# Maxima and exponentials of opposite row halves in turn, and three and two PSUM banks for them

## What is computed

```
xn = layernorm(x)
x + attn(xn) + ffn(xn)

attn: 16 heads of 8; softmax attention in chunks of 16 tokens, once on neighbours,
      once on every third token; the sum of both through Wo
ffn:  y  = xn + mla(rmsnorm(xn, w_ln1))          16 heads, causal, 512 x 512 scores
      y + moe(rmsnorm(y, w_ln2))                 1 shared and 7 routed experts, top 2

mla:  scores = einsum('bqhd,bkhd->bhqk', qq, kk) * scale, masked where k > q
      probs  = softmax(scores);  y = einsum('bhqk,bkhd->bqhd', probs, v) @ W_o
```

## Time and profile before

| | us |
|---|---|
| median of 3 runs | 514.09 |
| lowest, highest | 512.26, 516.3 |
| the profiled execution | 514.96 |
| its span on the chip | 513.0 |

### The profile page before, as it was taken

The page is one execution under the profiler, slowest core; times in us unless marked ns, Lnnn a source line. Parts: engine busy times, 40 slices in busy tenths (PEclk is TensorE's granted clock), DMA queues, the critical chain, the costliest instruction groups (busy, mean ns, idle before and its releaser), DMA issues.

```text
span 513.0 us, 11641 instructions
## 1 busy us (share of the span) xinstructions
PE 464.1 (90%) x4428; PEld 244.8 (48%) x4428; DVE 361.0 (70%) x1049; ACT 265.1 (52%) x486; POOL 53.2 (10%) x52
## 2 busy tenths in 40 slices
PE   3774988999999999999999997999999999987995
PEld 2322343445453555545455554454545545654652
DVE  6463586687767877776577784666677775688886
ACT  6252447457766554877754385776543444212110
POOL 4231001141001121010002120000010000010000
PEclk9868699999999999999999997999999999999899
DMA  6156000156000227100001264000400000000000
GB/s 206 24 137 116 0 3 2 21 127 134 3 2 3 65 56 134 27 3 2 2 3 34 54 125 68 1 3 2 125 1 4 2 1 22 0 22 1 1 20 21
DMA packets 18198, 20.22 MB, mean 39 GB/s; under 512 B 2824, under 2 KB 16392, under 8 KB 17352
## 3 DMA queue, kind: packets, MB, share of 16 engines
q1 hardware_dynamic: 18144, 19.49, 17.4%
HBM read 10.84 MB, written 7.47 MB: 36 GB/s over the span
## 4 chain that ended last, share of the span: by engine, by line
PE 60%; DVE 20%; DMA 6%; issue 5%; ACT 5%; SPq 3%; POOL 1%; DVEq 0%; ACTq 0%; POOLq 0%
PE bank_A L1080 7%; PE bank_c L1043 6%; PE bank_A L1001 6%; PE bank_B L1026 6%; PE bank_M L1091 6%; DVE x L942 4%; PE bank_B L1124 4%; DMA q_stack<-in_c_rows 4%; PE bank_M L1098 4%; DVE k_diag L922 3%; PE bank_B L1031 3%; PE bank_M L985 3%; DVE k_diag L927 3%; PE bank_A L1130 2%; SPq L478 2%
## 5 line engine op out<-in xcount | busy, mean ns | idle before, releaser
L672 ACT ACTIVATE p_mla<-bank_B 128x512 f32<-128x512 f32 (+1 forms) x176 | 97.5, 561 | 92.9 <-PE bank_B L1031 91.4
L819 DVE CUSTOM_DVE_ANT_0 differences<-masks,bank_A 128x384 bf16<-128x384 bf16 (+1 forms) x128 | 78.4, 613 | 25.2 <-PE bank_A L1001 20.2
L651 ACT ACTIVATE pT_loc<-sT_loc 32x512 f32<-32x512 f32 x136 | 85.1, 625 | 4.8 <-DVE sT_loc L845 3.4
L1001 PE MATMUL bank_A<-k_stack,q_stack 50*128 50x128 bf16 (+3 forms) x256 | 65.2, 307 | 11.0 <-DMA q_stack<-in_c_rows 7.4
L1124 PE MATMUL bank_B<-xrT,k_diag 128*128 128x512 f32 x128 | 64.4, 617 | 3.9 <-DVE k_diag L922 3.2
L1026 PE MATMUL bank_B<-q_stack,k_stack 50*128 50x512 bf16 (+3 forms) x256 | 63.9, 302 | 0.6 <-DVE k_diag L922 0.2
L838 DVE TENSOR_REDUCE row_max<-bank_A 128x16 f32<-128x512 f32 (+1 forms) x36 | 24.8, 690 | 40.7 <-PE bank_A L1080 40.6
L1080 PE MATMUL bank_A<-k_diag,qT 128*32 128x512 f32 x272 | 50.5, 772 | 0.0
L1031 PE MATMUL bank_B<-masks 64*128 64x64 bf16 (+1 forms) x512 | 50.3, 202 | 0.0
L1043 PE MATMUL bank_c<-p_mla,v_mla 128*9 128x128 f32 (+3 forms) x512 | 47.5, 442 | 0.4 <-ACT p_mla L672 0.3
L1031 PEld LDWEIGHTS bank_B<-masks 64*128 64x128 bf16 x512 | 39.8, 95 | 14.3 <-issue 0.2
(11 more groups left out here) (135 smaller groups left out, 593.3 us busy)
## 6 DMA issues: line engine op xcount, KB each, us to landing
parts_dram<-parts SPq DMA_DIRECT2D x16, 192.0 KB, 2.7
k_stack<-parts_dram SPq DMA_DIRECT2D x8, 384.0 KB
q_stack<-parts_dram SPq DMA_DIRECT2D x8, 384.0 KB
parts_dram<-parts SPq DMA_DIRECT2D x16, 128.0 KB, 2.7
k_diag<-kT SPq DMA_DIRECT2D x64, 18.0 KB
x<-in_x SPq DMA_DIRECT2D x4, 256.0 KB, 6.6
parts_dram<-parts SPq DMA_DIRECT2D x16, 64.0 KB, 2.3
out<-x SPq DMA_DIRECT2D x4, 256.0 KB, 2.2
```

The lines of the kernel that those rows point to most:

```text
L651: last = nc.scalar.activation(pT_loc[rows, :, rows], sT_loc[rows, t % 2, :].rearrange("p (h k) -> p h k", h=H), ACT.Exp, scale=SCALE)
L672: drained_by(nc.scalar.activation(p_mla[:, n % P_RING, m:m + len(heads), j * P:], src, ACT.Exp, scale=SCALE), step)
L819: drained_by(nc.vector.tensor_tensor_reduce(differences[:, 0:w], masked16[:, S - w:], bank[:, 0:w], -1.0, -NEG, ALU.add, ALU.min, dst), step)
L1001: last = nc.tensor.matmul(bank[:, n * w:(n + 1) * w], q_stack[b % 2][rows, h % 8, i * P:(i + 1) * P], k_stack[b % 2][rows, h % 8, 0:w], st ...
```

## The change

Ring A gets three banks and ring B two. The groups go in the order 0, 1, 2, 3 and a group's maxima units start with the widest tile, so that its 11 units have the same widths and head counts, one by one, as its 11 exponential units. The lists of maxima and exponentials become one, `scores`, over all 16 groups, spread evenly from -0.29 to 4.0: unit k of group n's maxima stands directly before unit k of the exponentials of group n - 2, followed by a PV where one is due. SHIFT of a group comes after the second unit of the next. `merged` takes such a bundle as one entry, so no other step comes between its parts.

On TensorE, where an exponential unit directly follows a maxima unit (`beside`), the maxima step only waits for its bank. The exponential step waits for its own and then issues both: exponential matmul of a head, maxima matmul of a head, in turn, and after them the masks in turn. The outputs and the norm of the third batch are placed somewhat later. No matmul, drain or DMA is added or taken away. The helpers `exp_matmul`, `exp_mask` and `half_of` (not shown) issue the matmuls of L1026 and L1031 with their operands as before.

```diff
--- before
+++ after
-BANKS = {"A": 2, "B": 3, "M": 2}
+BANKS = {"A": 3, "B": 2, "M": 2}
...
-GROUP_ORDER = [0, 2, 1, 3]
+GROUP_ORDER = [0, 1, 2, 3]
+LEAD = 2
...
 def score_units():
     units = []
     for g in GROUP_ORDER:
-        for i in range(NT):
+        for i in reversed(range(NT)):
...
-    "latent": [(0, 1.12), (1.12, 2.02), (2.02, 2.86), (2.86, 4)],
-    "maxima": [(-0.29, 0.63), (0.61, 1.44), (1.56, 2.46), (2.49, 3.54)],
+    "scores": [(-0.29, 4.0)],
...
-    "outputs": [(1.18, 1.34), (2.12, 2.26), (2.86, 2.97), (4.02, 4.27)],
-    "norm": [(1.31, 1.53), (2.33, 2.54), (3.17, 3.65), (4.28, 4.57)],
+    "outputs": [(1.18, 1.34), (2.13, 2.26), (3.08, 3.19), (4.02, 4.27)],
+    "norm": [(1.31, 1.53), (2.33, 2.54), (3.26, 3.65), (4.28, 4.57)],
...
-    def maxima(b):
-        steps = []
-        for n, g in enumerate(GROUP_ORDER):
-            steps += [("S", b, u) for u in range(PER_GROUP * n, PER_GROUP * n + PER_GROUP)] + [("SHIFT", b, g)]
-        return steps
-
-    def latent(b):
-        steps, late = [], []
-        for g in GROUP_ORDER:
-            for j in range(NT):
-                units = [("E", b, g, j, u) for u in range(len(exp_units(g, j)))]
-                steps += units[:1] + late + units[1:]
-                late = [("PV", b, g, j)]
-        return steps + late
+    def scores():
+
+
+        groups = [(b, g) for b in range(B) for g in GROUP_ORDER]
+        found, shift, late = [], [], []
+        for n in range(len(groups) + LEAD):
+            here = groups[n] if n < len(groups) else None
+            back = groups[n - LEAD] if n >= LEAD else None
+            exps = [("E",) + back + (j, u) for j in range(NT) for u in range(len(exp_units(back[1], j)))] if back else []
+            for k in range(PER_GROUP):
+                unit = []
+                if here:
+                    unit.append(("S", here[0], PER_GROUP * GROUP_ORDER.index(here[1]) + k))
+                if back:
+                    unit.append(exps[k])
+                found.append(unit + late + (shift if k == 1 else []))
+                late = []
+                if back and (k + 1 == PER_GROUP or exps[k + 1][3] != exps[k][3]):
+                    late = [("PV",) + exps[k][1:4]]
+            shift = [("SHIFT",) + here] if here else []
+        return found + [late]
...
-    lists = [(experts(range(B)), *at["experts"][0])]
+    lists = [(experts(range(B)), *at["experts"][0]), (scores(), *at["scores"][0])]
     for b in range(B):
-        lists += [(latent(b), *at["latent"][b]), (maxima(b), *at["maxima"][b]), (local(b), *at["local"][b]),
+        lists += [(local(b), *at["local"][b]),
                   (outputs(b), *at["outputs"][b]), (norm(b), *at["norm"][b]), ([("ST", b)], *at["stacks"][b]),
...
+    beside = {e: s for s, e in zip(steps, steps[1:]) if (s[0], e[0]) == ("S", "E")}
+    waits_for_e = set(beside.values())
...
+            def maxima_matmul(step, n):
+                b, (i, heads) = step[1], UNITS[step[2]]
+                h, w = heads[n], (i + 1) * P
+                rows = slice(half_of(h).start, half_of(h).start + STACK_ROWS)
+                return nc.tensor.matmul(bank_of(step)[:, n * w:(n + 1) * w],
+                                        q_stack[b % 2][rows, h % 8, i * P:(i + 1) * P],
+                                        k_stack[b % 2][rows, h % 8, 0:w], start=n == 0, stop=i >= 2,
+                                        skip_group_check=True)
+
+            def maxima_mask(step, n, low):
+                i, heads = UNITS[step[2]]
+                w = (i + 1) * P
+                return nc.tensor.matmul(bank_of(step)[:, (n + 1) * w - P + low * SLOT:(n + 1) * w],
+                                        half_eye[half_of(heads[n]), low, :],
+                                        half_causal[half_of(heads[n]), low, low * SLOT:], start=False, stop=True,
+                                        skip_group_check=True)
+
...
+                    if step not in waits_for_e:
+                        for n in range(len(UNITS[step[2]][1])):
+                            last = maxima_matmul(step, n)
+                        if UNITS[step[2]][0] < 2:
+                            for n in range(len(UNITS[step[2]][1])):
+                                for low in range(2):
+                                    last = maxima_mask(step, n, low)
+                        full_by(last, step)
...
+                    other = beside.get(step)
+                    for m in range(len(exp_units(g, j)[u])):
+                        exp_matmul(step, m)
+                        if other:
+                            last = maxima_matmul(other, m)
+                    if other and UNITS[other[2]][0] >= 2:
+                        full_by(last, other)
                     for m in range(len(exp_units(g, j)[u])):
                         for low in range(2):
-                            last = nc.tensor.matmul(bank[:, m * w:m * w + SLOT * (low + 1)], half_eye[half_rows, low, :],
-                                                    half_causalT[half_rows, low, 0:SLOT * (low + 1)],
-                                                    start=False, stop=True, skip_group_check=True)
-                    full_by(last, step)
+                            done = exp_mask(step, m, low)
+                            if other and UNITS[other[2]][0] < 2:
+                                last = maxima_mask(other, m, low)
+                    full_by(done, step)
+                    if other and UNITS[other[2]][0] < 2:
+                        full_by(last, other)
```

40 lines of the change are left out of this document (16 added, 24 removed).

## The result

| | before | after |
|---|---|---|
| median of 4 runs, us | 515.19 | 542.09 |
| lowest, highest | 512.26, 519.08 | 535.59, 547.23 |
| ratio, with 95% interval | | 1.0439 (1.029 to 1.0587) |
| the profiled execution, its span | 514.96, 513.0 | 547.23, 545.2 |
| mean granted clock of its span | 0.963 | 0.924 |

What follows compares the result with a forecast made beforehand. TensorE's own instruction stream was taken as the bound up to about 440 us. From 514.96 us, 28 us of pairing and fewer changes of kind came off and 9 us for two exponential banks went on: 496 us, range 482 to 512.

Steps and rivals of the forecast that it cites:

- Part 1: TensorE's score matmuls: 154 pairs on opposite halves overlap, 0.40 us instead of 0.62 for 512 columns; 32.8 us left to gain.
- rival (d): Pairs on TensorE: the halves don't overlap when interleaved by heads; 529 us, chance 0.02.
- Parts 1 and 2: TensorE's stream, about 365 us long: pairing saves 32.8 us and fewer changes of kind 4, together 37 us.
- Part 2: TensorE's changes of kind: unbroken runs of units fall from 208 to 176, 0.19 us each; 6.1 us at most, 4 taken.
- Part 3: Mixed stages: three quarters of TensorE's shorter stream, 28 us of 37, arrives, as present waits are small and VectorE and ScalarE aren't full.
- at least a third arrives: Mixed stages: lower bound on the gain that arrives, 12 us, if four fifths busy is as full as VectorE gets.
- Part 5: Moved steps: shift through DRAM, lead of nine units, third batch's outputs and norm; cost 0, shift bounds -2.6 and +5 us.
- Part 4: Experts beside exponentials: two banks for exponentials and gate/up hold TensorE 0.7 us for each of 12 experts; 9 us cost, bounds 7 to 18.
- the row it spoke of: Experts beside exponentials: waits on bank B from L922 and L927's successors, some 0.6 us each, a dozen times.
- Rival (c): Pairs: maxima units held until ScalarE, maybe in its 2.5 us block, drains the exponentials' bank, TensorE behind; 522 us, chance 0.11.
- Rival (b): Mixed stages: drains become the bound, VectorE's units leaving TensorE waiting for bank A; 12 us arrive, 512 us, chance 0.14.

Runs made afterwards that it cites:

- the best kernel: Changed kernel with PV one pair later and two banks for ring A, two for B, three for M: 510.36 us, 0.9852 of the kernel before.

## Why the prediction was wrong

**Part 1, the pairing: right.** 0.40 us for a pair, masks hidden, no delay of the second matmul; rival (d) is out.

**Parts 1 and 2, the stream 37 us shorter: somewhat too large.** With clocks near the old one the busy time fell by 29.1, 30.0 and 32.7 us (435.0, 434.1, 431.4 against 464.1). With 0.4 us taken off for each further us at half clock that is 31 to 34. In the changed kernel itself only 13 are seen, since it ran 44 us more at half clock, which is some 18 by the same estimate. Busy time counts overlapping matmuls once, so this is near, not equal to, what part 1 counts. Part 2's price of a change compared two different groups of eight matmuls (128x7 and 128x128), and no run tests it by itself.

**Part 3, how much of it arrives: the step that failed.** It took the small waits of the earlier trace rows and the free shares of VectorE and ScalarE to mean that three quarters of the gain, 28 us, would come through. None did: the changed kernel stands still for 45 us more (PV 13, ring M 23, ring B 9), and the lower clock takes some 18 more. Small waits at the old pace say that every result arrives before it is asked for. They don't say by how much. For PV the leads are measured: a median of 1.5 us before and 0.9 after. For ring M the reason is argued only. TensorE got faster while ScalarE and VectorE did not, so a lead of the same number of steps is shorter in time; but the old kernel with the new places alone, whose stream is not faster, already has 8 of ring M's 23 us. The bounds were wrong too: "at least a third arrives" came from an engine's share, and the loss came at a VectorE share of 69%. In the Trainium skill, "TensorEngine Tiling (Array Packing)", section PSUM Bottleneck warns that emptying PSUM may become the bottleneck. The runs agree in that the new waits that have a name are for VectorE or ScalarE, and differ in that neither engine is near full (69% and 59% of that stretch): it is when they get to a step, not their rate.

**Part 5, what is moved: incomplete.** It looked at the shift, the outputs and the norm and priced them at 0, which holds: from 75 to 480 us the changed kernel has no wait for a shift's readback or for the stacks. (The lead of nine units is some 40 steps, not 50, and 16 to 27 us, not 22 to 26.) It left out the steps that the bundle moves. PV now follows directly on a pair, 1.7 steps nearer to its exponentials; this costs 3.7% (521.05 against 542.09); in the profiled executions it is 12.5 us of idle time and 16 us of busy time, the latter as the clock was low for longer. And ring M, of whose two banks SHIFT takes one, wasn't costed at all. Its waits rose by 23 us, and a third bank for it gave back 2%.

**Part 4, two banks for ring B: right.** 9 forecast; 6.8 measured in the old order for the stretch meant, 1.56% (8 us) in all. In the changed kernel the row it spoke of is there, the second of PE's waits above: 11 waits for the gate's product, 7.9 us, 0.7 each, as forecast.

**Rival (c)** had the right direction and the right actor, ScalarE's block of 2.5 us with TensorE behind it, and the wrong place: the pair waited for ScalarE's exponentials 2.6 us in 4 waits, PV 13.1 in 11. Rival (b), the drains as bound, is nearest to what the rest is, but by order and not by share, and mostly for ring M, where it named ring A; it was put at 512 since its gain was taken to be at least 12 us.

**What stays open.** Why ring M's waits rise, by the faster stream or by the new places; why pairs at the old pace gave nothing beyond their 7 us at a shift; and 25 us of idle time that the best kernel still has over the kernel before. Ring A's waits are 14 of them and ring B's 11. By stretches it reaches the first expert at 357.4 us, 19.4 earlier than before, and then needs 73.3 us to the last exponential unit instead of 60.6. So more than half of the shorter stream does arrive up to the experts, and 13 us of it are lost beside them. The new places alone lengthen that stretch by 7 us (67.9, with 37 exponential units in it instead of 31) and two banks for ring B alone by 7 (67.4). That these two are the 13 is likely, but no run shows it.

## What to carry to other kernels

When all engines walk one ordered list, small waits and free shares don't say how much a shorter stream of the bound engine will give: before predicting a gain, take each step that reads another engine's result or reuses a bank, and measure in us how long before its start the result was there. A step moved into a bundle needs the same look, and so does each ring that the change doesn't touch. A bank is worth what its ring waits for in the new order, less what the ring that gives it will wait: a third bank for ring M, taken from ring A, was worth 2% with pairs and, taken from ring B, cost 1.4% without. And count the records before comparing busy times: 30 missing matmuls looked like 8 us gained.

## What the chip showed that was not expected

Stops of 2 to 4 us in a busy stream were mostly followed by half clock. In the changed kernel, busy us before and after the stop of 2.63 us that ended at 343.72 (the clock is the number before the DMA share):

```profile
336.00:342.00 6.00, 3.50 (x61) 2.13 (x58) 5.06 (x15) 3.33 (x7) 0.00 (x0) 1.00 0.01 3
344.00:350.00 6.00, 5.53 (x28) 1.64 (x22) 1.84 (x3) 1.08 (x3) 0.00 (x0) 0.51 0.01 3
```

and the same matmuls on either side of it, timeline of PE:

```profile
340.67 0.33 PE L986 MATMUL bank_B<-q_stack,k_stack 50*128 50x384 bf16 x1
340.84 0.25 PE L992 MATMUL bank_B<-masks 64*128 64x64 bf16 x2
343.72 1.90 PE L1081 MATMUL bank_c<-p_mla,v_mla 128*9 128x512 f32 x8 [2.63 <-ACT p_mla L681]
346.09 1.94 PE L1118 MATMUL bank_A<-k_diag,qT 128*32 128x512 f32 x8 [0.47 <-issue]
347.96 0.50 PE L986 MATMUL bank_B<-q_stack,k_stack 50*128 50x384 bf16 x1
348.25 0.36 PE L992 MATMUL bank_B<-masks 64*128 64x64 bf16 x2
```

The granted clock goes from 1.00 to 0.51, that is from 2.4 to 1.2 GHz, and a score matmul from 0.33 to 0.50 us. Between 75 and 480 us the changed kernel has nine such stretches, and seven of them begin within 1.5 us of the end of a stop of 1.6 to 3.8 us (ends at 76.7, 121.0, 172.3, 239.9, 304.9, 343.7 and 438.1). The kernel before has two, at its two longest stops (2.6 us up to 315.6, 3.0 up to 474.4). It isn't a rule: of the changed kernel's eleven such stops four were not followed by one (2.1 us up to 228.7, and those up to 319.0, 333.3 and 338.9), and two of its nine stretches (from 100.7 and 326.0) follow no such stop. All four runs of the changed kernel had a mean clock of 0.921 to 0.936. The Trainium skill, "TensorE: Matmul & The Clock Gate", section "A second HAM failure mode: psum-queue depth-cycling", describes frequent short idle times of TensorE that make its clock swing between the two levels; the trace agrees (82.7 us at the lower level against 38.4). What it cost can be estimated from the same 4428 matmuls: busy time of 451 us with 82.7 at half clock, 435.0 with 42.8. It does not simply follow the idle time, though: with ring M's third bank the changed kernel stood still almost as long (90.6 us) and had 41.8 us at half clock. And much of it comes early. From 46 us on, before the first exponential unit, one stretch lasted 23.9 us in the changed kernel and 10.2 in the kernel with PV one pair later, whose steps are the same up to there. No edit here explains that difference.
